# Mamba stage: two places per chunk for h, sums six chunks behind, products u and scaled tiles on VectorE, norm and skip at other states

## The reference, cut to what matters

```
xn = x * rsqrt(mean(x*x) + 1e-6) * g
x_s, z = split(xn @ W_in.T)
xc = silu(causal_conv4(x_s) + conv_b)
B_coef, C_coef, log_dt = split(xc @ W_x.T)
dt = softplus(log_dt @ W_dt.T + b_dt)
A_bar = exp(dt * A)                  # per token, channel and state
Bu = dt * B_coef * xc
h = A_bar * h + Bu                   # step by step over the tokens
y = sum over states of h * C_coef
y = (y + xc * D) * silu(z)
x = layernorm(x + (x + y @ W_out.T))
```

## Time and profile before

| | |
|---|---|
| median of 3 runs | 4149.21 us |
| profiled execution | 4151.48 us |
| its span | 4149.7 us |
| first to last scan of the stage | 1324.5 to 3224.7 us |
| groups 1 to 14 | 1441.6 to 3132.6 us, 120.8 us each |

### The profile page before, as it was taken

How to read it: one execution, slowest core, us unless ns; L and a number is a source line. 1 busy time by engine, 2 the same in 40 slices (tenths; PEclk the granted TensorE clock), 3 DMA queues, 4 the chain that set the end, 5 groups by cost and what they waited for, 6 DMA issues and landing times. The chain is left out here.

```text
span 4149.7 us, 72605 instructions
## 1 busy us (share of the span) xinstructions
PE 3428.0 (83%) x22048; PEld 2459.9 (59%) x22080; DVE 3109.4 (75%) x5211; ACT 2822.8 (68%) x5137; POOL 2714.2 (65%) x2890
## 2 busy tenths in 40 slices
PE   8996999989745888888888888888888699994666
PEld 5664666675423667666666766666667466662333
DVE  5666888844684788788877878887788487886988
ACT  2224777733565888887888888788888266664766
POOL 1224777600483898898988889898889365662555
PEclk9998999979867999999999999999999799997999
DMA  1111212151121111111111111111111121112110
GB/s 61 56 53 50 51 47 51 39 112 41 29 68 49 40 52 52 46 52 47 55 47 48 52 46 53 47 53 46 50 46 53 37 51 49 46 42 74 47 49 33
DMA packets 284832, 209.66 MB, mean 51 GB/s; under 512 B 131209, under 2 KB 249545, under 8 KB 284505
## 3 DMA queue, kind: packets, MB, share of 16 engines
q1 hardware_dynamic: 284504, 205.72, 17.8%
HBM read 149.18 MB, written 51.41 MB: 48 GB/s over the span
## 5 line engine op out<-in xcount | busy, mean ns | idle before, releaser
L2253 DVE TENSOR_TENSOR_SCAN ma_h<-ma_a,ma_pbu 128x512 f32<-128x512 f32 x1024 | 1223.6, 1210 | 342.1 <-PE ma_pbu L1851 165.5
L2149 POOL TENSOR_TENSOR ma_ch<-ma_h,ma_crep 128x512 f32<-128x512 f32 x1024 | 1335.8, 1320 | 204.5 <-DVE ma_h L2253 190.2
L1851 PE MATMUL ma_pbu<-ma_ident,ma_bu 128*128 128x128 f32 x4096 | 659.3, 285 | 171.1 <-DVE ma_h L2253 141.8
L1851 PEld LDWEIGHTS ma_pbu<-ma_ident,ma_bu 128*128 128x128 f32 x4096 | 486.0, 145 | 409.4 <-DVE ma_h L2253 285.5
L1860 PE MATMUL ma_py<-ma_ident,ma_ch 128*128 128x128 f32 x4096 | 647.3, 283 | 46.5 <-POOL ma_ch L2149 30.2
L2047 ACT ACTIVATE ma_a<-ma_dt,ma_A 128x510 f32<-128x510 f32 x1024 | 653.1, 717 | 1.2 <-issue 1.2
L2038 ACT ACTIVATE ma_bu<-ma_uT,ma_b_t 128x512 f32<-128x512 f32 x864 | 556.8, 719 | 10.2 <-PE ma_pbu L1851 8.5
L1860 PEld LDWEIGHTS ma_py<-ma_ident,ma_ch 128*128 128x128 f32 x4096 | 498.0, 146 | 77.2 <-POOL ma_ch L2149 64.7
L881 POOL TENSOR_TENSOR xa_prob<-xa_e,xa_rec_head 128x616 f32<-128x616 f32 x256 | 306.1, 1216 | 282.9 <-DVE xa_rec_head L971 282.8
L962 DVE TENSOR_REDUCE xa_top<-xa_pS 128x8 f32<-128x616 f32 x256 | 201.0, 785 | 134.9 <-PE xa_pS L650 132.0
L785 ACT ACTIVATE xa_e<-xa_low 128x616 f32<-128x616 f32 x256 | 184.9, 722 | 92.0 <-DVE xa_low L963 92.0
(11 more groups left out here) (313 smaller groups left out, 7276.0 us busy)
## 6 DMA issues: line engine op xcount, KB each, us to landing
ma_crep<-ma_ct_dram SPq DMA_DIRECT2D x256, 256.0 KB, 3.1
xa_x<-act SPq DMA_DIRECT2D x64, 256.0 KB, 2.9
act<-xa_y SPq DMA_DIRECT2D x64, 256.0 KB, 2.1
la_x<-in_x SPq DMA_DIRECT2D x32, 256.0 KB, 2.7
act<-la_y SPq DMA_DIRECT2D x32, 256.0 KB, 2.2
ea_x<-act SPq DMA_DIRECT2D x32, 256.0 KB, 12.0
act<-ea_x SPq DMA_DIRECT2D x32, 256.0 KB, 4.0
ma_x<-act SPq DMA_DIRECT2D x16, 512.0 KB, 4.6
```

What stands on the lines that cost most here:

```text
L1851: last = pe.transpose(pbu[c % 2][:, t * P:(t + 1) * P], bu[:, s % 2, t, c * P:(c + 1) * P], ident[:, :])
L2149: pool.tensor_tensor(ch[:, s % 2, c], h[:, c], crep[:, s % 4, :], ALU.mult).then_inc(multiplied, 1)
L2253: dve.tensor_tensor_scan(out=h[:, c, :], data0=a[:, s % 2, c, :], data1=pbu[c % 2][:, :], initial=0.0, op0=ALU.mult, op1=ALU.add).then_inc ...
```

## The change

`h` gets two places per chunk, by the parity of the state. The scan's wait for `multiplied` is unchanged in its text, and the count starts at 8 in place of 4. The sums on PE come six steps behind the turning in place of five, and at the head of a group the new group's sums start at step 9 with two per step until they have caught up. The buffer `yv` now shares the place of `one_av`. The product `u` moves from POOL to DVE. The table `on_pool` (one tile of ten states) becomes two tables: 10 tiles on DVE, 8 on POOL, so 46 of 64 tiles stay on ACT where 54 were. The skip product comes at states 10 and 12 in place of 6 and 10, the second half of the output at (8, 3) to (9, 3) in place of (8, 1) to (9, 0), statistics and finish of the group before some steps apart from each other, squares of the norm spread over states 2 to 4 (its rms at step (6, 2) and diagonal at (7, 1) on POOL). B is turned into `pm[0]` two states later and no longer stands in the way of the output projection.

```diff
+    LAG = 6
-        h = sb("h", [P, IC, GS])
+        h = sb("h", [P, 2, IC, GS])
-        yv = sb("yv", [P, IC, GS])
+        yv = one_av
-        def on_pool(s):
-            return 1 <= s <= 10
+        DVE_TILES = {1: 1, 7: 2, 8: 1, 9: 1, 10: 1, 11: 1, 13: 1, 14: 1, 15: 1}
+        POOL_TILES = {2: 1, 3: 1, 4: 1, 5: 1, 6: 1, 8: 1, 9: 1, 10: 1}
...
@@ tensor
-                pe.wait_ge(multiplied, K * g + (IC * s + c + 5))
+                pe.wait_ge(multiplied, K * g + (IC * s + c + 9))
...
-                if t == 2 and piece == 0:
-                    if prep:
-                        pe.wait_ge(b_copied, g + 3)
-                    else:
-                        pe.wait_ge(y_ready, 2 * g + 1)
+                    pe.wait_ge(y_ready, 2 * g + 1)
...
-                        late = IC * s + c - 5
-                        if late >= 0:
-                            sum_state(g, late // IC, late % IC)
+                        at = IC * s + c
+                        if at < LAG and not first:
+                            late = K - LAG + at
+                            sum_state(g - 1, late // IC, late % IC)
+                        for _ in range(2):
+                            if at >= LAG + 3 and done <= at - LAG:
+                                sum_state(g, done // IC, done % IC)
+                                done += 1
...
@@ scalar
-                for t in range(TT - 1 if on_pool(s) else TT):
+                for t in range(TT - DVE_TILES.get(s, 0) - POOL_TILES.get(s, 0)):
...
@@ gpsimd
-            pool.sem_inc(multiplied, IC)
+            pool.sem_inc(multiplied, 2 * IC)
-                        if prep and (s, c) in ((11, 1), (12, 0), (12, 3), (13, 2)):
-                            step_input(n, 1 - par, (4 * s + c - 44) // 3, 0)
-                        if prep and (s, c) in ((11, 2), (12, 1), (13, 0), (13, 3)):
-                            step_input(n, 1 - par, (4 * s + c - 45) // 3, 1)
-                        if (s, c) in ((6, 2), (10, 0)) and not first:
+                        if prep and (s, c) in INPUTS:
+                            step_input(n, 1 - par, INPUTS[s, c])
+                        if (s, c) in ((6, 1), (10, 3)) and not first:
                             rstd_of(g - 1, 0 if s == 6 else 1)
...
@@ vector
+            def step_input(n, par, c):
+                dve.wait_ge(dt_ready, IC * n + (c + 1))
+                dve.tensor_tensor(u[:, c, :], dt[:, par, c, :], xc[:, par, c, :], ALU.mult).then_inc(u_ready, 1)
...
-                dve.tensor_tensor_scan(out=h[:, c, :], data0=a[:, s % 2, c, :], data1=pbu[c % 2][:, :],
+                dve.tensor_tensor_scan(out=h[:, s % 2, c, :], data0=a[:, s % 2, c, :], data1=pbu[c % 2][:, :],
...
+                dve.tensor_scalar(bu[:, s % 2, t, :], uT[:, par, t, :], b_t[:, par, t, s:s + 1], None,
+                                  ALU.mult).then_inc(dve_tile_ready, 1)
...
+            STATS = {(5, 2): 0, (5, 3): 1, (10, 0): 2, (10, 1): 3}
+            INPUTS = {(13, 0): 0, (13, 1): 1, (13, 3): 2, (14, 0): 3}
+            FINISH = {(7, 0): 0, (7, 1): 1, (11, 2): 2, (11, 3): 3}
```

More of the change, by code:

```diff
@@ L1741, in group @@
                         store_c(g + 1, 1 - par)
-                    if s == 8 and not first:
+                    if s == 9 and not first:
                         store_y(g - 1, 0)
@@ L1820, in spread_l, with turn_b @@
                 pe.matmul(pm[0][:, :], ones[:, :], ct[0:1, :], start=True, stop=True).then_inc(l_made, 1)
[L1822 to L1827, removed]
+            def turn_b(n):
+                pe.wait_ge(l_used, 2 * n + 2)
                 for t in range(TT):
-                    last = pe.transpose(pm[1][:, t * P:(t + 1) * P], ct[:, t * P:(t + 1) * P], ident[:, :])
+                    last = pe.transpose(pm[0][:, t * P:(t + 1) * P], ct[:, t * P:(t + 1) * P], ident[:, :])
                 last.then_inc(b_made, 1)
@@ L1952, in _ @@
             groups(pe, group)
-            for late in range(K - 5, K):
+            for late in range(K - LAG, K):
                 sum_state(NG - 1, late // IC, late % IC)
@@ L1970, in copy_z, with squares @@
                 act.activation(sz[:, par, t, :], pm[1][:, :], ACT.Copy).then_inc(z_copied, 1)
-            def squares(n):
+            def squares(n, tiles):
                 act.wait_ge(x_loaded, 16 * n + 16)
-                for t in range(TT):
+                for t in tiles:
                     act.activation(square[:, t, :], x[:, t, :], ACT.Square, accum_out=ssq[:, t:t + 1]).then_inc(ssq_ready, 1)
@@ L2061, in group @@
                             copy_xT(n, c)
[L2062 to L2065, removed]
+                    if s in SQUARES and ahead:
+                        squares(g + 2, SQUARES[s])
+                    if s in (3, 4) and not first:
+                        copy_gated(g - 1, 2 * s - 5)
                     if s == 7 and prep:
                         copy_parameters(n)
-                    if s == 8 and prep:
-                        copy_b(n, np_)
                     if s == 9 and prep:
@@ L2102, in _ @@
             link(act.activation(A[:, :, :], A[:, :, :], ACT.Copy, scale=-1.0))
-            squares(0)
+            squares(0, range(TT))
             act.wait_ge(setup_done, 1)
@@ L2109, in _ @@
                 copy_z(0, 0, t)
-            squares(1)
+            squares(1, range(TT))
             silu_x(0, 0)
@@ L2202, in _ @@
             for c in range(IC):
-                for k in range(2):
-                    step_input(0, 0, c, k)
+                step_input(0, 0, c)
             rms_of(1)
@@ L2289, in group @@
                     for c in range(IC):
-                        if not first and (s, c) in ((0, 3), (1, 0)):
-                            for t in (2 * s, 2 * s + 1):
+                        if not first and (s, c) in ((1, 2), (1, 3)):
+                            for t in (2 * c - 4, 2 * c - 3):
                                 gate(g - 1, 1 - par, t)
@@ L2333, in _ @@
                     take_lost(0, c)
+            for c in range(IC):
+                step_input(0, 0, c)
             groups(dve, group, link, turns=NG // 2 - 2)
```

151 lines of the change are left out of this document (88 added, 63 removed).

## The result

The changed kernel takes 4076.14 us in the median of 4 runs (4074.91 to 4076.36), against 4149.93 of the kernel before on the same chip: a ratio of 0.9815, 95% interval 0.9803 to 0.9826. The forecast was 4070 with a range of 4000 to 4150. The first scan starts at 1326.8 and the last at 3148.5; groups 1 to 14 take 115.6 us each (forecast 115.6), group 0 109.7 (117.1 before), group 15, which prepares no next one, 94.8 to the end of its last scan (93.3).

The account below looks back on a forecast made before the run. No engine fills the group; a ring of scan, product with C, sum and next scan bounds it. DVE's 105.9 us of work plus 9.7 idle give 115.6 per group, 5.2 less over 15 groups: 4070 us, range 4000 to 4150.

Parts of the forecast that it names:

- idle terms: DVE's remaining waits per group: PE 6.4 us, ACT 1.5, POOL 1.0, rstd 0.5, small rest 0.3; 9.7 in all.
- u on DVE: Four products u moved to DVE at 0.90 us each add 3.6 us per group; similar row take_lost had 0.972.
- Tiles on DVE: Ten tiles moved to DVE add 6.0 us per group, at 0.60 us each as union.
- POOL's price: 14 more DVE operations lengthen POOL's by 0.3 us each, 4.2 per group; POOL then has 104.5 us.
- point 1: With two places for h, POOL may lag further; the scan's wait for its product falls from 7.6 to 1.0 us per group.
- Points 2 to 4: Waits per group: rstd 3.1 to 0.5 us; PE 10.4 to 6.4, without B's copy and u; ACT's decay 2.7 to 1.5.
- Tiles as relief for ACT: ACT loses 8 of 54 tiles at 0.645 us each, 5.2 us per group.
- B's condition: Rival, chance 0.22: POOL keeps its 13.3 us of idle beside 104.5 of work; group 117.8 us, time 4104.
- D's price: Rival, chance 0.14: meeting POOL, DVE's 14 new operations cost up to 22.5 us per group; slower, about 4195 us.
- E's mechanism: Rival, chance 0.08: PE's sum waits for POOL and blocks the next turning, so h's second place does nothing; 4150 us.
- C's 110.9 us per group: Rival, chance 0.13: a looser ring takes up nearly every local mismatch, 105.9 plus 5 us per group; time 4003.

Follow-up runs that it names:

- The four together: Two places for h, u on DVE, B's turning moved and the output's norm spread out, all in the kernel before: 4155.4 us, 1.0012.
- the kernel where it was tested: Changed kernel with only the tiles of states 7 to 9 on DVE (4045.4 us); with the old head of a group put back: 4073.2 us.

## Why the prediction was right, and where it was not

*Time.* The group took 115.6 us as forecast. That exactness is luck: DVE's work was 103.5 us where I had 105.9, and its idle time 12.1 where I had 9.7. Of the idle terms, PE's was 8.6 us where I had 6.4, ACT's 2.25 for 1.5, POOL's 0.9 for 1.0 and `rstd`'s nothing for 0.5.

*u on DVE.* Right: 0.956 us for 0.97, from the row of the same kind and size. The figure goes with the order: with no tiles on DVE the same products took 1.226 us and `take_lost` 0.716 in place of 0.99.

*Tiles on DVE.* Too dear: 0.491 us in the mean for 0.67, 68.7/14 = 4.9 us per group by the row. In the sum's measure, DVE's busy time, they are worth 4.2 us per group for 6.0, by the kernel that has none of them on DVE. The length without a wait was right (0.46 for 0.42 to 0.47); the wait of 0.25, read from `one_plus`, was not there. Who meets POOL's operation is a matter of phase, not of how busy POOL is. In state 13 of one group, DVE and then POOL (start, us):

```profile
2107.33 0.66 DVE L2263 TENSOR_TENSOR ma_av<-ma_dt,ma_xc 128x512 f32<-128x512 f32 x1
...
2109.04 0.46 DVE L2279 TENSOR_SCALAR ma_bu<-ma_uT,ma_b_t 128x512 f32<-128x512 f32 x1
2109.42 1.77 DVE L2263 TENSOR_TENSOR ma_av<-ma_dt,ma_xc 128x512 f32<-128x512 f32 x1
```

```profile
2107.38 1.75 POOL L2179 TENSOR_TENSOR ma_dt<-ma_dt,ma_gT 128x512 f32<-128x512 f32 x1
2109.09 3.22 POOL L2167 TENSOR_TENSOR ma_ch<-ma_h,ma_crep 128x512 f32<-128x512 f32 x2
```

The tile at 2109.04 starts 0.05 us before POOL's product with C and takes its bare 0.46. The product u at 2109.42 finds that POOL operation 0.3 us old and takes 1.77, as `take_lost` did in the earlier trace rows. At this place u takes 1.76 or 1.77 us in each of the 15 groups that prepare a next one.

*POOL's price.* Right: product with C 1.369 us (forecast 1.35), POOL 104.3 us per group (104.5).

*Waits, point 1: h's place.* This step failed. The wait fell as forecast (7.6 to 0.9 us per group), but not by the place: without the place it is as short (13.0 us over the 14 groups), and with the place alone it turns into a wait for PE. What takes it away is the move of u, with the steps that come with it: with that alone, and one place, it fell from 106.8 to 19.4 us. The prediction held both facts (the sum blocks the turning; POOL sheds u) and gave the gain to the wrong one.

*Points 2 to 4.* In the changed kernel the waits for `rstd`, for the copy of B and for u went as I said; the scan's waits for PE and for ACT fell less. In the kernel before none of these parts alone was worth its size, since another wait stood behind: ACT's decay at (9, 0) behind B's and at (15, 0) behind u's, and waits for PE and POOL behind `rstd`'s. My sum took DVE's idle time as a list from which entries can be struck. The four together took 3.3 us per group off it, where my terms for their waits come to 13.2 (6.6, 2.6 and 4.0), and they gave no time at all. And I had no term for the head of the group, which I had called moved with nothing gained: it is worth 28 us in the kernel where it was tested. The order counted where I charged it with nothing.

*Tiles as relief for ACT.* I took 5.2 us from ACT as good. Six of the ten tiles cost more than they brought; if the relief is worth something, it is in states 7 to 9 alone.

*Rivals.* B's condition nearly held, POOL idles 11.3 us per group for its 13.3, though the group is 2.2 shorter than B's. D's price was far off: its 22.5 us for the fourteen operations are 8.7 by their rows. E's mechanism is real for the place of h. C's 110.9 us per group was not reached here, nor by any kernel above.

*Open.* Measured at the changed kernel or next to it: u 34 us, head 28, division of tiles -20, place of h 0. They add up to 42 of the 75, which is an account only as far as the parts are independent, and the waits above say that they are not. Measured in the kernel before: u 10, four parts together 0. Not tried apart are the steps of z and of u's copies on ACT and PE, the squares, the exponentials and logarithms, and the skip; B's turning and the norm's spread were tried in the kernel before alone. That ACT's order is what held the four parts back is what their waits point to; it is not shown.

## What to carry to other kernels

Idle time by its releaser says which wait ended last, not what would end next: before a wait is struck from a sum, look one or two steps on for the engine that is ready just behind it. In a ring of engines that run in fixed order, a second buffer may only move the wait to the next in-order engine, as it did here while POOL's work stayed the same. A wait struck from the sum can also come back as longer work, where two engines hold each other up. And work given from one engine to another for balance should be tried state by state: six tiles hurt, four helped at most a little.

## What the runs showed of the hardware that was not expected

DVE and POOL take turns on operations with SBUF operands of these kinds at the grain of a whole instruction, and the cost depends on who comes first. Where `one_plus`, `lost_part`, `take_lost`, u or a tile started with over 0.15 us of a 128x512 POOL operation left, it took its bare length plus what was left of that operation, less 0.10 to 0.17 us: 221 times over both kernels, without an exception. With less than that left it took its bare length to within 0.1 us. So u took 0.66 to 1.77 us and a tile 0.452 to 1.272. The scans, with one operand in PSUM, met POOL's products all the time and took 1.18 to 1.22 us, all 1024 of them. Where POOL comes second, its operation is longer in its place: `dt` took 1.613 us in the mean after the change, 1.405 before, 1.27 undisturbed. That one meeting lines the two engines up, so that the next operations pay little, is a reading of these traces; no run set the phase by itself.

The Trainium skill (SBUF — State Buffer, section SBUF: two separate sides) has whichever of the two starts first hold the shared pair of ports for the whole instruction, the other blocked. The 1.77 us of u and the 1.613 of `dt` agree with that. The estimate of 0.33 us for a tile that the prediction worked out from the Trainium skill (VectorE: DVE Perf Modes, section The TRN2 errata) lies under the 0.452 of the shortest one here.

In every kernel here the first scan after a turn of the hardware loop waited 2.3 to 4.6 us (2.7 to 3.2 before, 2.6 to 2.8 after the change); no edit took that wait away. At one such turn, in the kernel with the tiles of states 7 to 9 on DVE, PE had idled 3.0 us, and the granted clock was 0.51 over the next 3 us, the 1.2 GHz level: groups of four 128x128 matmuls took 1.06 to 1.11 us there and 0.60 where the clock was full.
